# Two-layer attention kernel: the first layer's running maxima in tiles of 128 queries, dealt one pair a place

## What is computed

```python
px = avg_pool_3x3_s2(x)                     # 28 x 28 = 784 tokens
qt = conv1x1(x, w_qs, b_qs)                 # 8 heads of 16
kt = conv1x1(px, w_qs, b_qs); vt = conv1x1(px, w_vs, b_vs)
q = qt.reshape(B * 8 * 2, 8, N).transpose(0, 2, 1)   # two mixtures a head, 8 channels each
attn = softmax(einsum('bnd,bdk->bnk', q, kt.reshape(B * 8 * 2, 8, 784)) / 4, axis=2)
attn = (attn * pi).reshape(B * 8, 2, N, 784).sum(1)
out = conv1x1(attn @ vt, w_out) * inv * gamma + beta + x
```

## Time and profile before

| | us |
|---|---|
| median of 3 runs | 4899.85 |
| lowest, highest | 4897.66, 4905.59 |
| the profiled execution | 4941.7 |
| its span, first to last instruction | 4939.7 |
| PE matmuls busy | 4250.2 (86%) |
| DVE busy | 2960.9 (60%) |
| ACT busy | 2420.8 (49%) |
| POOL busy | 517.8 (10%) |

### The profile page before, as it was taken

One profiled execution on the slowest core, in us unless ns is written; L12 is line 12 of the kernel. 1 busy time (PEld: TensorE's weight loads), 2 busy tenths in 40 slices (PEclk: granted clock), 3 DMA queues, 4 the chain that ended last, 5 costly groups with the idle time before them and its releaser, 6 DMA issues.

```text
span 4939.7 us, 69414 instructions
## 1 busy us (share of the span) xinstructions
PE 4250.2 (86%) x27098; PEld 1111.1 (22%) x27098; DVE 2960.9 (60%) x8660; ACT 2420.8 (49%) x2830; POOL 517.8 (10%) x819
## 2 busy tenths in 40 slices
PE   7755378888888888799989999999999999999998
PEld 2111011221212122222222222222222222222222
DVE  5433255555555555577766776667767667776771
ACT  3322134444444445425555556655555555555555
POOL 2101212111121211111000000000000000000000
PEclk6555555555555556669999999999999999999999
DMA  1499910000000020012222222222232222232321
GB/s 41 29 57 56 61 14 12 9 12 7 12 12 9 12 58 12 5 32 70 67 66 67 57 79 68 74 56 68 69 83 59 75 58 73 63 80 56 85 56 36
DMA packets 262672, 236.15 MB, mean 48 GB/s; under 512 B 215129, under 2 KB 218057, under 8 KB 262089
## 3 DMA queue, kind: packets, MB, share of 16 engines
q1 hardware_dynamic: 241544, 205.85, 22.7%
q0 software_dynamic: 20800, 25.87, 2.5%
HBM read 226.65 MB, written 27.19 MB: 51 GB/s over the span
## 4 chain that ended last, share of the span: by engine, by line
PE 75%; DMA 9%; DVE 8%; issue 5%; ACT 1%; POOL 1%; SPq 0%; POOLq 0%; ACTq 0%; DVEq 0%
PE P L588 23%; PE P L573 14%; PE P L535 12%; PE P L540 6%; PE P L554 6%; PE P L614 4%; DVE maxes L879 4%; DMA d_den<-sums 4%; PE P L558 4%; PE P L653 3%; DMA d_rden<-rden 2%; DVE junk L875 2%; DMA rwide<-d_rden 2%; DVE q_stack L912 1%; DMA den<-d_den 1%
## 5 line engine op out<-in xcount | busy, mean ns | idle before, releaser
L757 ACT ACTIVATE probs<-P 128x896 f32<-128x896 f32 (+1 forms) x2352 | 2124.7, 916 | 2017.2 <-PE P L573 1136.6
L875 DVE CUSTOM_DVE_ANT_0 junk<-P,mstage 112x448 bf16<-112x448 f32 x3136 | 1780.3, 621 | 757.0 <-PE P L535 756.5
L588 PE MATMUL P<-probs,vals 128*17 128x448 f32 (+1 forms) x9408 | 1381.7, 666 | 27.0 <-ACT sums L837 26.8
L879 DVE TENSOR_REDUCE maxes<-P 112x1 f32<-112x392 f32 x1792 | 898.5, 559 | 753.1 <-PE P L540 752.5
L540 PE MATMUL P<-keys,q_stack 24*112 24x392 f16 x1792 | 567.7, 513 | 400.6 <-DVE maxes L879 261.4
L573 PE MATMUL P<-bstage,flip 112*56 112x448 f16 x6272 | 905.0, 369 | 0.0
L535 PE MATMUL P<-keys,q_stack 48*112 48x448 f16 x3136 | 755.9, 408 | 121.8 <-DVE q_stack L912 51.2
L554 PE MATMUL P<-q_two,keys 49*128 49x448 f16 x3136 | 649.0, 358 | 0.0
L535 PEld LDWEIGHTS P<-keys,q_stack 48*112 48x112 f16 x3136 | 281.0, 126 | 1030.8 <-DVE maxes L875 493.3
L423 POOL DMA_DIRECT2D d_den<-sums x84 | 49.5, 589 | 3081.2 <-ACT sums L837 3081.2
L573 PEld LDWEIGHTS P<-bstage,flip 112*56 112x56 f16 x6272 | 212.2, 105 | 589.1 <-issue 589.1
(11 more groups left out here) (124 smaller groups left out, 1520.2 us busy)
## 6 DMA issues: line engine op xcount, KB each, us to landing
mstage<-g_max SPq DMA_DIRECT2D x56, 1519.0 KB, 7.9
bstage<-g_bias SPq DMA_DIRECT2D x28, 1568.0 KB, 8.2
bstage<-g_bias SPq DMA_DIRECT2D x28, 1519.0 KB, 7.8
rwide<-d_rden POOLq DMA_DIRECT2D x336, 56.0 KB, 2.1
g_max<-t_bf SPq DMA_DIRECT2D x16, 673.8 KB
g_bias<-t_hi SPq DMA_DIRECT2D x8, 679.9 KB
g_bias<-t_lo SPq DMA_DIRECT2D x8, 679.9 KB
wg<-in_wg POOLq DMA_DIRECT2D x12, 386.0 KB, 3.3
```

Of the source, the lines that this page charges most:

```text
L588: last = mm(P[32 * h:32 * h + HD + 1, PV, 0:QB], table[0:kr, kt, h, :], probs[0:kr, s % 3, h, :], start=kt == 0, stop=kt == unit.tiles - 1 ...
L757: A(probs[0:kr, s % 3, 2 * p:2 * p + 2, :], P[0:kr, 2 * p:2 * p + 2, 0:QB], ACT.Exp).then_inc(exp_done, 1)
L875: V.tensor_tensor_reduce(out=junk[:, PLAN.nth[job] % 4, :], in0=P[0:QT, bank_of(job), 0:QB], in1=bias, scale=1.0, scalar=-3.0e38, op0=ALU. ...
L879: V.tensor_reduce(out=maxes0[:, unit.i % 2, t, 2 * p + r, c:c + 1], in_=P[0:QT, bank_of(job), 0:HALF], op=ALU.max, axis=AX.X).then_inc(max ...
```

## The change

- The first layer's first pass uses tiles of QT0 = 128 queries. The seven units of a group are taken two by two: an even unit has four tiles, of which the last takes 64 of its queries and 64 of the next unit's; the odd unit behind it has three, from its query 64 on. The last unit of a group (u = 6) has four, the last with 64 queries. A group has 25 tiles instead of 28.
- The order within a tile is p = 1, then p = 0.
- `window`: an odd unit's 12 pairs go over 6 steps, an even unit's 16 over 8; u = 0 keeps 7 steps for its 16 pairs.
- The q job stands six steps ahead of the previous unit's start for odd u, four for even, three before.
- `q_stack` becomes one buffer of four slots, so that a tile can reach from a unit's queries into the next unit's; `maxes0` and `negmax0` are doubled; the turn of an odd unit takes its first 64 queries from the previous unit's last tile. It has five products as before.
- Before the last tile of an even unit (u < 6) PE waits for the next unit's q.

```diff
+QT0 = 128
-            self.work ... else [(p, t, c) for t in range(TILES) for c in range(2) for p in range(2)])
+        self.wide = 3 + (self.u + 1) % 2
+        self.tile0 = QT0 // 2 * (self.u % 2)
+        self.slot = 2 * ((4 * self.group + self.u // 2) % 2) + self.u % 2
+        self.work = [(p, t, c) for t in range(self.wide) for c in range(2) for p in (1, 0)]
+
+    def queries(self, t):
+        return QT0 // 2 if self.u == ROWS8 - 1 and t == 3 else QT0
...
+    def window(self, unit):
+        first, end = self.start(unit.i - 1) - 1, BASE[unit.i] - 1
+        if not unit.biased and 0 < unit.u < ROWS8 - 1:
+            return (first, end - 1) if unit.u % 2 else (first - 1, end)
+        return first - (not unit.biased and unit.u > 0), end
...
-            places = [(s, w) for s in range(self.start(unit.i - 1) - 1, BASE[unit.i] - 1) for w in "ab"]
+            places = [(s, w) for s in range(*self.window(unit)) for w in "ab"]
...
-            at = self.start(i - 1) - 3
+            at = self.start(i - 1) - (3 if unit.biased else 6 if unit.u % 2 else 4)
...
-        q_stack = [sb(f"q_stack{k}", [128, 2, QB], F16) for k in range(2)]
+        q_stack = sb("q_stack", [128, 4, QB], F16)
...
+                elif not unit.biased and (p, t, c) == (1, 3, 0) and unit.u < ROWS8 - 1:
+                    pe.wait_ge(stacked, 1 + PLAN.nth["q", unit.i + 1, 0])
...
-                        mm(o, q_stack[unit.i % 2][rows, 0, t * QT:(t + 1) * QT],
+                        at, size = unit.slot * QB + unit.tile0 + t * QT0, unit.queries(t)
+                        mm(P[0:size, bank_of(job), 0:HALF], q_flat[rows, at:at + size],
                            keys0[unit.group % 2][rows, c * HALF:(c + 1) * HALF], start=True, stop=True)\
...
+                    if unit.tile0:
+                        mm(P[:, bank, 0:QT0 // 2], negmax0[:, (i - 1) % 2, 3, :], eye16[:, QT0 // 2:QT0], start=False,
+                           stop=True, skip_group_check=True)
+                    for t in range(unit.wide):
+                        size, at = unit.queries(t), unit.tile0 + t * QT0
+                        width = min(size, QB - at)
+                        last = mm(P[:, bank, at:at + width], negmax0[0:size, i % 2, t, :], eye16[0:size, 0:width],
+                                  start=False, stop=True, skip_group_check=True)
...
-                        V.tensor_reduce(out=maxes0[:, unit.i % 2, t, 2 * p + r, c:c + 1], in_=P[0:QT, bank_of(job), 0:HALF],
+                        V.tensor_reduce(out=maxes0[0:size, unit.i % 2, t, 2 * p + r, c:c + 1],
+                                        in_=P[0:size, bank_of(job), 0:HALF], op=ALU.max, axis=AX.X).then_inc(max_done, 1)
...
-                    V.tensor_reduce(out=negmax0[:, :, 24::32], in_=maxes0[:, unit.i % 2, :, :, :], op=ALU.max, axis=AX.X,
+                    n = unit.wide
+                    V.tensor_reduce(out=negmax0[:, unit.i % 2, 0:n, 24::32], in_=maxes0[:, unit.i % 2, 0:n, :, :],
```

More of the change, by code:

```diff
@@ L63, in __init__ @@
         self.keys = 128 if self.biased else QT
-        self.work = ([(p, t, c) for p in range(2) for t in range(TILES) for c in range(7)] if self.biased
-                     else [(p, t, c) for t in range(TILES) for c in range(2) for p in range(2)])
+        if self.biased:
+            self.work = [(p, t, c) for p in range(2) for t in range(TILES) for c in range(7)]
+            return
+        self.wide = 3 + (self.u + 1) % 2
[4 more added lines that the diff above has]
+        return QT0 // 2 if self.u == ROWS8 - 1 and t == 3 else QT0
 UNITS = [Unit(i) for i in range(FIRST1 + NB * GROUPS1 * ROWS8)]
@@ L194, in build @@
         junk = sb("junk", [QT, 4, QB], BF16)
-        maxes0 = sb("maxes0", [QT, 2, TILES, 4, 2])
+        maxes0 = sb("maxes0", [QT0, 2, 4, 4, 2])
         maxes1 = sb("maxes1", [QT, 2, TILES, 2, 7])
-        negmax0 = sb("negmax0", [QT, TILES, 128], F16)
+        negmax0 = sb("negmax0", [QT0, 2, 4, 128], F16)
         negmax1 = sb("negmax1", [QT, 2, TILES, 128], F16)
@@ L263, in build @@
         ident = eye16[0:QT, 0:QT]
+        q_flat = q_stack[:, :, :].rearrange("k a n -> k (a n)")
         mean = cst[:, C_MEAN:C_MEAN + 128]
@@ L531, in first_pass @@
                     free(job)
-                    o = P[0:QT, bank_of(job), 0:QB if unit.biased else HALF]
                     if unit.biased:
+                        o = P[0:QT, bank_of(job), 0:QB]
                         rows = slice(64 * r, 64 * r + 48)
-                        mm(o.rearrange("q (a n) -> q a n", n=W), q_stack[unit.i % 2][rows, p, t * QT:(t + 1) * QT],
+                        mm(o.rearrange("q (a n) -> q a n", n=W), q_stack[rows, 2 * (unit.i % 2) + p, t * QT:(t + 1) * QT],
                            key_columns(unit.group, p, c, rows), start=True, stop=True).then_inc(scores_made, 1)
@@ L639, in turn_maxima @@
                 bank = bank_of(job)
[L640 to L643, removed]
+                slot = 2 * (i % 2) + p if unit.biased else unit.slot
+                mm(P[:, bank, 0:QB], eye16[:, :], q_stack[:, slot, :], start=True, stop=False, skip_group_check=True)
+                if unit.biased:
+                    for t in range(TILES):
+                        last = mm(P[:, bank, t * QT:(t + 1) * QT], negmax1[:, p, t, :], ident, start=False, stop=True,
+                                  skip_group_check=True)
+                else:
+                    if unit.tile0:
[6 more added lines that the diff above has]
+                                  start=False, stop=True, skip_group_check=True)
                 last.then_inc(neg_turned, 1)
@@ L878, in first_pass @@
                     else:
-                        V.tensor_reduce(out=maxes0[:, unit.i % 2, t, 2 * p + r, c:c + 1], in_=P[0:QT, bank_of(job), 0:HALF],
-                                        op=ALU.max, axis=AX.X).then_inc(max_done, 1)
+                        size = unit.queries(t)
+                        V.tensor_reduce(out=maxes0[0:size, unit.i % 2, t, 2 * p + r, c:c + 1],
+                                        in_=P[0:size, bank_of(job), 0:HALF], op=ALU.max, axis=AX.X).then_inc(max_done, 1)
                 if unit.biased and k + 1 in (len(unit.work) // 2, len(unit.work)):
@@ L890, in first_pass @@
                         dve.wait_ge(neg_turned, PLAN.nth["s", unit.i - 1, 0] + 1)
-                    V.tensor_reduce(out=negmax0[:, :, 24::32], in_=maxes0[:, unit.i % 2, :, :, :], op=ALU.max, axis=AX.X,
-                                    negate=True).then_inc(neg_made[0], 1)
+                    n = unit.wide
+                    V.tensor_reduce(out=negmax0[:, unit.i % 2, 0:n, 24::32], in_=maxes0[:, unit.i % 2, 0:n, :, :],
+                                    op=ALU.max, axis=AX.X, negate=True).then_inc(neg_made[0], 1)
             def stack(job):
@@ L902, in stack @@
                 if job[0] == "q":
-                    o, bias = q_stack[job[1] % 2][:, p, :], biases[k][:, A_Q + p:A_Q + p + 1]
+                    unit = UNITS[job[1]]
+                    slot = 2 * (unit.i % 2) + p if unit.biased else unit.slot
+                    o, bias = q_stack[:, slot, :], biases[k][:, A_Q + p:A_Q + p + 1]
                 else:
@@ L1025, in _ @@
             V.memset(P[:, PV, :], 0.0)
-            V.memset(negmax0[:, :, :], 0.0)
+            V.memset(negmax0[:, :, :, :], 0.0)
             V.memset(negmax1[:, :, :, :], 0.0)
```

## The result

The changed kernel takes 4783.6 us (median of 4, 4765.7 to 4796.5) against 4902.5 before: a ratio of 0.9728, interval 0.9696 to 0.9759 (the two medians alone give 0.976). On another chip it came to 4781.1 and 0.9729 (0.9714 to 0.9744). The forecast was 4780. So the gain is 119 us by the medians of the first chip and 133 us by either ratio.

What follows compares the result with a forecast made beforehand. PE was taken to set the regular stretch's pace, with a wait each step for a bank DVE must empty. Gains of 100 + 9 + 11 = 120 us take 4899.85 to 4780 us; range 4730 to 4820.

Steps and rivals of the forecast that it cites:

- turn: Turn of the maxima in step 6 of a unit, five matmuls; the step was put at 3.93 us, 5.15 before.
- Regular stretch: From 640 to 1910 us, 39 units in which PE sets the pace; claimed gain 100 us.
- plain step: Step from one start of the values to the next, one pair a place and no extra job; put at 3.46 us.
- steps 6, 0, 1 and 2: Numbered steps within a group's last unit, put at 5.15, 5.56, 5.56 and 5.75 us.
- doubled places: Places in a step that carry two pairs instead of one; each priced at 0.95 us.
- late order: Steps with p=0 first, whose first product starts later (0.36 against 0.09 us); right order priced at 0.27 us.
- The starting unit of 32.70 us: Seven steps read from one unit before the change, clock never raised; 39 such units were said to fill 640 to 1910 us.
- Under the DMA load: From 230 to 640 us, round trips of the denominators set the pace; claimed gain nothing, bounds 0 and 22 us.
- Early and late: Units in 60 to 230 us and 1910 to 2150 us; about 2.5 us each, so 9 and 11 us gained.
- The clock rival: The long uninterrupted run around the turn lifts the clock once more a unit: 39 to 50 us more, 4735; chance 0.15.
- the waits: Rival: PE really waits for the three banks, so 58 us of the gain are given back, 4838 us; chance 0.12.
- The overlap of wide tiles with the scores: Rival: 128-query tiles do not run beside the scores, 230 us lost against 120 gained, 5010 us; chance 0.04.

Runs made afterwards that it cites:

- second profiles: Kernel before and changed kernel each run and profiled again, nothing altered: 4891.6 us before; 4781.1 us, ratio 0.9729, after.
- the placing: Changed kernel with every unit's pairs dealt over the same seven steps, so not one pair a place: 4829.4 us, 0.9826.
- the wide weights alone: Kernel before, with first-pass products of tiles 0 to 2 loading 128 query columns instead of 112: 4907.9 us, 0.9996.
- the cut of the values: Two of four value slots issued ahead of the step's second group of pairs, two behind: changed kernel 4570.7 us (0.9300), kernel before 5037.0 us (1.0264).

## Why the prediction was right

**Regular stretch, 100 us:** measured 89.5 in the second profiles and 105 in the first. The parts that were tried hold: plain step 3.38 for 3.46, turn 3.85 for 3.93, the order 70 us when undone for 65 to 75, the placing 48 for 40 (these two from the expectations of the runs). At the end of a group, in steps 6, 0, 1 and 2 with their doubled places and late order, the second profile has 5.33, 5.55, 5.55 and 5.89 us where 5.15, 5.56, 5.56 and 5.75 were forecast. "Each matmul still streams 392 columns and each reduction still reads 392: their price per instruction stays" was wrong for the loads, and the wide weights alone show 0.07 of the 0.08 us by which a plain step came out shorter. Against it the forecast missed the 64-query tile, 0.86 us in each of eight groups.

One sign of being right failed. PE's waits for the reductions were to fall by some 100 us and fell by 40 in the regular stretch. The sum had priced steps from start to start, and most of what they lost are products that stood in the chain beside the wait: the two more of a doubled place, and the 0.36 for 0.09 us of the late order. The reduction of 0.57 us stayed in each plain step. To call the gain a wait for DVE was the wrong name for a right sum. The sign of the units was rough as well: between copies of the sums the units of the second profile take 27.7 to 29.9 us on average (29 to 30 was forecast, and 32.4 for the last of a group, which took 29.9), but 31.0 in u = 5 and 33.7 in u = 4, where the keys and values of the next group are projected.

The starting unit of 32.70 us had no stretch at full clock in it. That 1270 / 39 gives the same is partly chance: in the second profile of before, units take 30.6 to 32.7 us, and the one in seven with the projections of keys and values 36.6.

**Under the DMA load, nothing:** 391.1 us became 396.1 and 397.5 became 398.7. The round trips of the denominators set the pace, and what PE gained is waited for: from 230 to 590 us the three transfers of each trip hold 58% of the changed kernel's chain, where they held 57% before.

**Early and late, 9 and 11 us:** the early term was mis-sized. They measured 19 and 17 in the second profiles. I had counted two and a half us a unit, for the doubles and a part of the order, but took no row of the early stretch. In the late one six units gain 2.9 us each; I had counted four and a half of them. In the early one a unit gains about twice the 2.5. There PE's busy time fell by 18 us, at a granted clock of 0.69 for 0.66; what of it is clock was not tested.

**The clock, unchanged:** 0.57 before and 0.55 after over the regular stretch. The clock rival, with 0.15, did not come in. "As many stretches as before" was a little too many: in the clock record of the second profiles the regular stretch has 50 stretches at full clock before (168 us) and 32 after (117 us), in the first profiles 40 and 32. By the forecast's own 1 us a stretch, an estimate, that cost 8 to 18 us, about the size of the shortfall from 100 to 89.5, though 10 us between single profiles can also be chance. And another grant was near: one more change in PE's order, the cut of the values, took it to 0.91.

**The sum:** 120 us forecast, 119 measured by the medians, 116 by the second profiles, 133 by the ratio (118 to 149) and also on the other chip (134 by its medians). So the forecast is 1 to 14 us off. That it is so near is in part luck, since an early and late excess of 16 met a shortfall of 10 in the regular stretch and 10 in the stretches that I held fixed.

**Rivals:** the waits did not move to the q bank or the turn (4.45 us behind a projection, 4.53 forecast). The overlap of wide tiles with the scores was not lost. It is lost for the one tile that is narrower, a case that the rival named for the wrong width.

## What to carry to other kernels

Where a ring of banks is refilled by a slower engine, ask which product frees the next one and start that first; swapping the order of two independent products was worth 70 us here. Price a step at both levels of the clock before moving work: the same cut of the values was worth -210 us in a kernel where the clock came up to 0.91, and +130 where it reached 0.63. Look at the remainder tile too: 64 columns did not run beside 112, while 128 did, and widening it to 128 cost no time here (0.9693 against 0.9729).

## What the runs showed of the hardware that was not expected

- Weights of 24 rows load in 118 ns with 128 columns and in 183 with 112, in one kernel. The Trainium skill (TensorE: Matmul & The Clock Gate, Weight-path perf modes) says that the fast load is on at 128 weights and types other than FP32; the trace agrees for this form. In the second layer, at nearly full clock, it does not show: 48 rows by 112 columns load in 126 ns and 49 by 128 in 125.
- Products of 64 columns did not run beside products of 112 on other rows of the array; this cost 0.43 us a step.
- Values for two slots, on two column strips, take nearly as long as for four on four: 1.61 us against 1.63 at half clock, 0.86 against 0.95 at full.
- The granted clock stayed half through uninterrupted work. In the kernel before with the cut, PE was busy for all of this stretch, with a projection in it (L615), at 0.50 (columns as above). What the grant wants beyond uninterrupted work is open.

```profile
1160.88:1174.40 13.52, 13.52 (x46) 2.34 (x48) 5.11 (x12) 4.49 (x6) 3.84 (x6) 0.50 0.08 18
```
